# A four-layer sequence kernel: score pairs of a step put together, attention results compacted by transfers, VectorE's side work spread over steps

## The reference

```python
x = x + _L0_attn_ref(_layernorm(x), w_q, w_k, w_v, w_o)      # 16 heads of 16, maxima in two blocks of 256 keys
x = x + _L0_ffn_ref(_layernorm(x), fast_b, w_fc, w_proj, u, v, gate)   # 256 -> 1024 -> relu squared -> 256, ternary weights
x = x + _L1_attn_ref(_layernorm(x), qkv_w, qkv_b, out_w, out_b)        # 16 heads, softmax
x = x + _L1_ffn_ref(_layernorm(x), W_in, b_in, W_out)        # 8 trees of depth 7: only nodes on the chosen path count
```

## Time and profile before

| | us |
|---|---|
| median of 3 runs | 3209.13 |
| lowest, highest | 3197.66, 3212.54 |
| the profiled execution | 3217.72 |
| its span (core 0, mean granted TensorE clock 0.963) | 3215.9 |

### The profile page before, as it was taken

One profiled execution on the slowest core, in us unless ns is written; L12 is line 12 of the kernel. 1 busy time (PEld: TensorE's weight loads), 2 busy tenths in 40 slices (PEclk: granted clock), 3 DMA queues, 4 the chain that ended last, 5 costly groups with the idle time before them and its releaser, 6 DMA issues.

```text
span 3215.9 us, 50344 instructions
## 1 busy us (share of the span) xinstructions
PE 2934.8 (91%) x19007; PEld 1329.9 (41%) x19007; DVE 2073.3 (64%) x3769; ACT 1918.7 (60%) x2899; POOL 1151.0 (36%) x1535
## 2 busy tenths in 40 slices
PE   4789999899988999889998999989998899998999
PEld 1233333257523333326742333333763233332476
DVE  7676766744567777754467677675447766767544
ACT  3666666654466666664446666666445666666644
POOL 4234443135313444214431344421442144442244
PEclk7799999999989999999989999999998999999999
DMA  4100000000100000000010000000010000000000
GB/s 146 35 22 22 22 22 26 18 1 27 47 25 26 24 22 22 22 12 14 30 36 27 25 24 22 22 22 7 14 44 27 27 22 22 25 19 26 2 14 14
DMA packets 90432, 82.62 MB, mean 26 GB/s; under 512 B 15531, under 2 KB 89651, under 8 KB 90179
## 3 DMA queue, kind: packets, MB, share of 16 engines
q1 hardware_dynamic: 90191, 79.40, 7.4%
HBM read 17.48 MB, written 8.39 MB: 8 GB/s over the span
## 4 chain that ended last, share of the span: by engine, by line
PE 71%; DVE 15%; ACT 5%; issue 4%; POOL 3%; SPq 1%; DMA 1%; ACTq 0%; DVEq 0%; POOLq 0%
PE ps L1064 20%; PE ps L1099 12%; PE ps L1129 12%; PE ps L1343 10%; PE ps L1070 5%; DVE nmax L827 5%; DVE nmax L824 4%; PE ps L1165 4%; ACT arena L617 2%; PE ps L1115 2%; PE ps L1076 2%; PE ps L1334 2%; DVE stats L776 1%; DVE hT L810 1%; POOL h L434 1%
## 5 line engine op out<-in xcount | busy, mean ns | idle before, releaser
L617 ACT ACTIVATE arena<-ps 128x1024 f32<-128x1024 f32 x684 | 699.8, 1023 | 541.6 <-PE ps L1115 539.2
L1099 PE MATMUL ps<-kst,qst 48*128 48x512 f16 x2048 | 750.9, 402 | 185.5 <-DVE nmax L824 100.3
L824 DVE TENSOR_REDUCE nmax<-ps 128x2 f32<-128x512 f32 x1024 | 667.6, 685 | 325.2 <-PE ps L1099 320.6
L827 DVE TENSOR_REDUCE nmax<-ps 128x1 f32<-128x512 f32 x1024 | 668.2, 685 | 299.8 <-PE ps L1099 298.5
L1115 PE MATMUL ps<-qst,kst 54*128 54x512 f16 x2048 | 748.4, 400 | 36.1 <-ACT arena L617 31.3
L1129 PE MATMUL ps<-arena,vn 128*32 128x512 f32 x4096 | 566.6, 627 | 0.2
L1099 PEld LDWEIGHTS ps<-kst,qst 48*128 48x128 f16 x2048 | 165.0, 94 | 957.5 <-DVE nmax L824 350.6
L614 ACT ACTIVATE arena<-ps 128x512 f32<-128x512 f32 x680 | 405.6, 596 | 111.6 <-PE ps L1115 109.4
L530 POOL TENSOR_TENSOR arena<-arena 127x512 f16<-127x512 f32 (+1 forms) x256 | 290.7, 1156 | 425.6 <-ACT arena L769 425.6
L1343 PE MATMUL ps<-wout,arena 127*128 127x256 f16 (+1 forms) x3072 | 356.9, 272 | 0.0
L1064 PE MATMUL ps<-hT,win 128*127 128x512 f16 (+1 forms) x1536 | 353.2, 379 | 1.4 <-ACT arena L617 1.4
(11 more groups left out here) (118 smaller groups left out, 3278.7 us busy)
## 6 DMA issues: line engine op xcount, KB each, us to landing
qst<-parts SPq DMA_DIRECT2D x384, 64.0 KB, 2.6
kst<-parts SPq DMA_DIRECT2D x384, 64.0 KB, 2.6
x<-in_x SPq DMA_DIRECT2D x16, 512.0 KB, 4.0
out<-x SPq DMA_DIRECT2D x16, 512.0 KB, 2.9
qst<-nrow SPq DMA_DIRECT2D x256, 12.0 KB
arena<-in_winT SPq DMA_DIRECT2D x1, 2040.0 KB, 8.9
arena<-in_wfcT SPq DMA_DIRECT2D x1, 1024.0 KB, 7.9
arena<-in_wprT SPq DMA_DIRECT2D x1, 1024.0 KB, 9.8
```

The source lines that it names most:

```text
L617: nc.scalar.activation(pr[:, lo:hi + 1:hi - lo, :], ps[:, 2:4, :], ACT.Exp).then_inc(exp_rd, 1)
L824: nc.vector.tensor_reduce(nmax[:, u, 2 * tt + half, :, slot], bank[tt % 2].rearrange("p (a s) -> p a s", s=BLK), AX.X, ALU.max, negate=Tru ...
L827: nc.vector.tensor_reduce(nmax[:, u, 2 * tt + half, 0, slot:slot + 1], bank[tt % 2], AX.X, ALU.max, negate=True).then_inc(max_rd, 1)
L1099: mm(bank[tt % 2], qst[lo:hi, n % 2, e // 2, tt * P:(tt + 1) * P], kst[lo:hi, n % 2, e // 2, :], start=True, stop=True).then_inc(max_ps, 1)
```

## The change

1. **Pairs.** The tensor block's side units move into a function `beside(b, i, s)`, which is called after pair 3. A step is now pair 0, pair 1, `weighted`, pair 2, pair 3, then all side units of the step one behind the other.
2. **Attention results.** `natural` and `attn_T` are gone. SyncE's queue has a new `att_up(n)` of 12 transfers: two write the four sum rows of a half of `oT`, each 16 times over, to a buffer `spread` in device memory (256 KB), eight copy the values of one head position (64 KB) into `raw_att` (the old `h`), features on the partitions, and two read `spread` into `den`, of the same shape. VectorE's `divided(n, k)` takes a reciprocal of 128 x 512 sums (L873) and multiplies 128 x 512 values by it (L875), for k = 0 after the maxima of step 6 and for k = 1 after those of step 7 (in the tree stage both at a = 3). ScalarE and VectorE take the high and low parts from `raw_att` at s = 8, 9 and 9, 10. The rows of the output weights are permuted on the host (`by_value`).
3. **Side work moved.** The units stand at other steps (table below); of VectorE's work the low parts of the feed-forward norm go from the end of a phase to step 0 of the next, `moments` from step 0 to step 1, `values` from steps 5 and 15 to steps 7 and 9 (at 7 behind `divided`), the residual additions from 12 and 13 to 11 and 12.
4. **Buffers.** `qk` has one buffer instead of two, so ScalarE's write of each waits for GpSimd's read of the last; `out_read` waits for the transfers of the phase before.

```diff
         @block.sync
+            def att_up(n):
+                for gh in range(2):
+                    sp.wait_ge(oT_sb, n * NG + 2 * gh + 2)
+                    if n:
+                        sp.wait_ge(att_in[gh], n * 80)
+                    sp.dma_start(spread[gh], sums(gh)).then_inc(den_out[gh], 16)
+                for gh in range(2):
+                    for j in range(G):
+                        rows = slice(gh * HALF + j * HD, gh * HALF + (j + 1) * HD)
+                        sp.dma_start(raw_att[rows], oT[32 * j:32 * j + HD, 2 * gh:2 * gh + 2, :]).then_inc(att_in[gh], 16)
+                for gh in range(2):
+                    sp.wait_ge(den_out[gh], n * 16 + 16)
+                    sp.dma_start(den[gh * HALF:(gh + 1) * HALF].rearrange("p k s -> p (k s)"),
+                                 spread[gh].rearrange("j r s -> (j r) s")).then_inc(att_in[gh], 16)
...
                     rows_up(n, 1)
                     if prep:
+                        sp.wait_ge(hT_ps, norm_at(b, norm_of(i + 1)) * KD + KD)
...
+                    if i:
+                        att_up(n - 1)
+                    if prep:
                         stack_up(n + 1, 0)
+                        stack_up(n + 1, 1)
                     rows_up(n, 2)
...
         @block.vector
-            def natural(n, tt, src):
-                nat = bank[src].rearrange("p (a c) -> p a c", c=2 * HD)
-                dve.wait_ge(nat_ps, n * T + (tt + 1))
-                nc.vector.reciprocal(rden[:, tt, :], nat[:, :, HD]).then_inc(rden_sb, 1)
-                dve.wait_ge(rden_sb, n * T + (tt + 1))
-                nc.vector.tensor_tensor(h[:, tt, :].rearrange("p (a d) -> p a d", d=HD), nat[:, :, 0:HD],
-                                        rden[:, tt, :].rearrange("p (a o) -> p a o", o=1).to_broadcast([P, H, HD]),
-                                        ALU.mult).then_inc(attn_sb, 1)
...
+            def divided(n, k):
+                for gh in range(2):
+                    dve.wait_ge(att_in[gh], n * 80 + 80)
+                nc.vector.reciprocal(den[:, k, :], den[:, k, :]).then_inc(rden_sb, 1)
+                dve.wait_ge(rden_sb, n * KD + (k + 1))
+                nc.vector.tensor_tensor(raw_att[:, k, :], raw_att[:, k, :], den[:, k, :], ALU.mult).then_inc(attn_sb, 1)
...
                     if ahead:
                         maxima(*ahead, (3,))
...
+                    if s == 1 and ffn:
+                        moments(b, nxt)
+                    if s in (6, 7) and post:
+                        divided(n - 1, s - 6)
+                    if s == 7 and biased:
+                        values(n + 1, 0, 6)
+                    if s == 9 and biased:
+                        values(n + 1, 1, 7)
+                    if s in (11, 12) and post:
+                        attn_residual(n - 1, s - 11, 7)
...
         @block.tensor
+            def beside(b, i, s):
...
+                if s == 7:
+                    if ffn:
+                        pe.wait_ge(v_sb, (n + 1) * 2 + 1)
+                        hidden(b, q, 7)
+                    if prep:
+                        if ffn:
+                            pe.wait_ge(relu_rd, f * M0 + 7)
+                        else:
+                            pe.wait_ge(mrow_sb, n * NG + 3)
+                        qk_unit(n + 1, 2, PREP_T, 7)
...
+                    for kt in (2, 3):
+                        if ahead:
+                            maxima(*ahead, kt)
+                        scores(b, i, s, kt)
+                    beside(b, i, s)
```

More of the change, by code:

```diff
@@ new lines, in beside @@
+                if s == 11:
+                    if ffn:
+                        ffn_out(f, 1)
+                    if post:
+                        pe.wait_ge(attn_upd, (n - 1) * 2 + 1)
+                        projected(n - 1, 1, POST_T, 7)
+                if s == 12 and ffn:
+                    pe.wait_ge(scl_mul, f * 2 + 1)
+                    ffn_out(f, 2)
+                if s == 13:
+                    if ffn:
+                        ffn_out(f, 3)
+                    if prep:
+                        if post:
+                            pe.wait_ge(attn_upd, (n - 1) * 2 + 2)
+                        else:
+                            pe.wait_ge(mrow_sb, n * NG + 4)
+                        maxima_rows(n + 1, 0)
```

525 lines of the change are left out of this document (239 added, 286 removed).

## The result

| | before | after |
|---|---|---|
| median of 3 runs, us | 3209.13 | 3495.68 |
| lowest, highest | 3197.66, 3212.54 | 3491.95, 3510.63 |
| ratio, 95% interval | | 1.091 [1.085, 1.098] |
| span of the profiled execution, mean granted clock | 3215.9, 0.963 | 3508.8, 0.91 |

The account below looks back on a forecast made before the run. TensorE's work was taken to bound the tree stage and feed-forward phases, VectorE's maxima to count in light phases. Biased phases +19.5 and the remaining stages summed to +17.5 us a quad, +70 in all: 3280 us, range 3150 to 3380.

Parts of the forecast that it names:

- The price of the reciprocal: On VectorE, one reciprocal of 128 x 512 was taken at 3.2 us; with multiplication and semaphore 3.9 us.
- The flat reading: Rival: the reciprocal of 512 is nearly flat, 0.76 us, total about 3150 us; chance 0.20.
- the dear one: Rival: the reciprocal of 512 costs 10.5 ns an element, 5.4 us, total 3400 us at the end; chance 0.20.
- Where it lands: Steps 6 and 7 of biased feed-forward phases: TensorE waits for values behind the second reciprocal, +8.9 us; i = 2, +4.5.
- The late transposes of step 2: Step 2 of feed-forward phases: moments end in step 1, so GpSimd's norm reaches TensorE's transposes 1.2 us late.
- The wait of step 9: Step 9 of biased feed-forward phases: waits for the second read of the values, 5.1 us instead of 2.4.
- I charge nothing: SyncE's transfers before the divisions: hidden with 4 us (feed-forward), 1 (phase 1) and -0.5 (phase 7) to spare.
- transfers are late: Rival: copies or spread land 3 us later, VectorE stands with all maxima behind; +84 at most, 3360 us; chance 0.10.
- The light phases and the tree stage: Each quad: phase 0 -3 us, phase 1 +1, phase 6 -1, phase 7 +3.5, tree stage -1.5.
- TensorE has some 10 us of other work: Tree stage: both divisions, 7.8 us, stand between a decision and its mask beside TensorE's other work; charged +1 us.
- The other 14 steps: Feed-forward phase without steps 6 and 7: waits sum to 9.0, 66.5 us against 70.6; -4.1 biased, -5.5 not.
- +1.7 each: Biased feed-forward phases: TensorE idles 5.6 us, then the lower clock loses some 1.7 us of its work per phase.

## Why the prediction went wrong, point by point

- **The price of the reciprocal: right.** Forecast 3.2 us, measured 3.35. The flat reading (0.76) and the dear one (5.4) are out. The Trainium skill, "VectorE: DVE Perf Modes", section "Walkthrough: the 8-slice pipeline in each mode", gives a repeat count of 8 and no time; the 4.3 us that I had estimated from it was right in that the price goes by the element, but 0.95 us too dear.
- **Where it lands: right.** A wait of 5 us before the matmul on wfc, measured 5.39; 64.7 us in 12 places. The late transposes of step 2, 1.2 us each, were in the sum too, and 44.6 us in 29 places are 1.2 each, when the one of 12.0 is taken off, which stood before as well (12.1). The wait of step 9 was taken at 2.7 (5.1 instead of 2.4) and measures 34.2 / 16 = 2.1. In the biased phases the mechanism was the one forecast, and each was 3 to 6 us dearer.
- **"I charge nothing" for the transfers: wrong.** This is the first step that failed. Issue was taken at 0.63 us for every transfer and landings at that of a 64 KB row, so the sums were to be there "with 4, 1 and -0.5 us" to spare (the items of that chain add up to 12.2, not 12.5). The copies took 1.0 to 1.45 us each to issue, the loads landed in 4.0 instead of 2.6, and VectorE waited in 22 of 32 places, 94.8 us; taking the transfers away gave 82. It is the rival "transfers are late", priced at +84 at most, which came true beside the forecast and not in its place, and more by slow issues than by the slow landing that it names. I had given it 0.10 as if one excluded the other.
- **The light phases and the tree stage: wrong.** This is the second step that failed. Of the 57.8 us that this quad took beyond the forecast, 36.0 lie in phases 1 and 7 and the tree stage. Late transfers are a part only: without any, phase 1 is 8.3 us above before (forecast +1), phase 7 9.7 (+3.5), the tree stage 5.7 (-1.5). I had counted a reciprocal there at its length less what is hidden, and no clock; in phase 7 the two cost 10.8 us against 5.6 of length, as the same matmuls ran at 0.82. The sentence "TensorE has some 10 us of other work" in the tree stage doesn't hold either: with no transfer in the way the two divisions still cost 6.2 us (215.5 against 209.3), and transfers 6.5 us late add 4.3.
- **"The other 14 steps": mis-sized.** Forecast 66.5 us in a biased phase; in the phase shown (i = 4, 90.9 us) they took 70.9. One wait was not in the list of 9.0 us (whose items add up to 8.2): the split of the maxima, 34.3 us in 16 places. Its move back gave 29. The order of GpSimd's queue shows it; I had followed the queues of VectorE and TensorE only. For i = 2, without the wait of step 9, the items would give -6.8 and not the -5.5 of the sum, so that phase, +5.6 instead of -1, was missed by more than it seems.
- **"+1.7 each" for the clock: too small, as far as the rows go.** In the phase shown the two units behind the wait alone lost 1.28 + 1.19 = 2.5 us. And the clock stayed or fell again at places without a wait of that size: behind the wait of step 9,

```profile
1319.18 0.39 PE L1147 MATMUL ps<-idb,npart 128*24 128x128 f16 x4 [2.03 <-DVE vn L854]
...
1321.61 1.94 PE L1171 MATMUL ps<-arena,vn 128*32 128x512 f32 x8
...
1324.44 3.11 PE L1197 MATMUL ps<-wpt,arena 128*128 128x256 f16 x16
```

`weighted` took 1.94 us instead of 1.07 and `ffn_out` 3.11 instead of 1.92 a step later (granted clock 0.51 in the 4 us from 1320.00, with one more wait, of 0.96 us, in them): 2.1 us more lost behind a wait of 2.0. Phase 7 has a mean clock of 0.79, where TensorE is idle for 29% of the time. Over the span, the part of full speed not granted is (1 - 0.91) x 3509 = 316 us against (1 - 0.963) x 3216 = 119; I had charged 1.7 x 12 = 20. How much of these 197 us counts isn't shown for the whole: a slow clock costs only where TensorE is the bound. In phase 7 TensorE's longer busy time is 7.6 of the 10.8 us that the reciprocals cost, by the two rows above.
- **The gain of the removed transposes: not shown.** 113 us were computed as the most they could be worth, and the kernel without the three costs is 110 us faster than before. The agreement is luck: by place the gain isn't where transposes went (phase 0: 7.2 us with none removed; tree stage: 0.5 with six sets).
- **The sum**, in us, against before: net gain of everything moved -110; late pieces +145 to +151 (forecast: part of the 9.0 us a phase); reciprocals and transfers together +245 to +251, of which taking out the transfers alone gives back 82 (forecast 0), the reciprocals alone 132, and 37 more go only with both. The forecast of +70 was right in sign, and the wait behind the values, its main mechanism, is there; it failed by what it put at nothing and by the light stages.

## What to carry to other kernels

Where a change takes work from the bounding engine and gives a long instruction to its supplier, price the new instruction by its elements, and then follow every queue that it passes for what now stands behind it: here three moves of existing work gave back 151 us. Rivals that name different resources aren't alternatives; their prices add, and here two of them added to 37 us more than their sum, in phases 1 and 6. A total that agrees with a count proves little until its places agree too. The issue times of a transfer chain should be taken from a trace with like transfers: a transfer that repeats a row should be measured before it is called hidden.

## What the runs showed of the hardware

- A reciprocal on VectorE takes 248 ns for 16 elements a partition, 1744 for 256 and 3346 for 512: 6.26 ns an element ((3346 - 1744) / 256) and some 0.14 us fixed. A multiplication of 512 takes 0.69 us.
- Copies queued behind transfers of 256 KB that read a row 16 times issue in 1.04 to 1.45 us each instead of 0.63 (8.32 to 11.60 us for eight). The same 16-fold repeat as a read from device memory left VectorE waiting 172.7 us instead of 94.8, but six issues behind it took 3.83 us, 0.64 each.
- Four rows of on-chip memory, each read 16 times, moved at 47 GB/s with a DMA share of 0.22, and row by row over more DMA engines at 46 GB/s with 0.90.
- The same 265 matmuls of a phase took 39.98 us at a granted clock of 1.00 and 47.59 us at 0.82.
- Behind a TensorE wait of 5.4 us two units ran at nearly twice their time (2.74 and 2.65 against 1.46 us), and some 2.4 us behind one of 2.0 us `weighted` and `ffn_out` did too.
